# Causal mask moved from TensorE matmuls into VectorE's extreme pass, and the last group's product moved one step, in a fused attention and expert block

## The reference

```python
x = L0_attn_x                                  # [8, 1024, 256] f32
xn = _layernorm(x, axis=-1)
x = x + _L0_attn_ref(xn, w_qkv, w_out) + _L0_ffn_ref(xn, wg, w1, b1, w2, b2)

# attention: 16 heads of 64, 8 batches of 1024 tokens
logits = einsum('bqhd,bkhd->bhqk', q, k) / sqrt(64)
logits = where(tril, logits, -0.7 * finfo(float32).max)
probs = softmax(logits, axis=-1)
out = einsum('bhqk,bkhd->bqhd', probs, v)      # then einsum('bshd,hde->bse', out, w_out)
# _L0_ffn_ref: a top-2 mixture of 8 experts with capacity 2048, hidden size 1024
```

## Time and profile before

| | |
|---|---|
| median of three runs | 3558.74 us |
| profiled execution | 3556.85 us |
| its span | 3555.0 us |
| mean granted TensorE clock over the span | 0.982 |
| attention stage, from and to | about 935 to 3555 us |
| one unit | 40.2 us |
| busy in the span: PE, PEld, DVE, ACT, POOL | 95%, 78%, 62%, 59%, 40% |

### The profile page before, as it was taken

One profiled execution on the slowest core, in us unless ns is written; L12 is line 12 of the kernel. 1 busy time (PEld: TensorE's weight loads), 2 busy tenths in 40 slices (PEclk: granted clock), 3 DMA queues, 4 the chain that ended last, 5 costly groups with the idle time before them and its releaser, 6 DMA issues.

```text
span 3555.0 us, 67268 instructions
## 1 busy us (share of the span) xinstructions
PE 3390.4 (95%) x24085; PEld 2763.0 (78%) x24085; DVE 2219.5 (62%) x4719; ACT 2104.2 (59%) x4500; POOL 1436.5 (40%) x2025
## 2 busy tenths in 40 slices
PE   5599999999799999999999999999999999999998
PEld 3489998999677777777777777777777777777776
DVE  5844444443367666666666666667666666666666
ACT  2345444444366666666666666666666666666664
POOL 2122221220133345554454444554445444455445
PEclk8799999999899999999999999999999999999999
DMA  5122222221311112221222112211122111221111
GB/s 189 43 67 72 72 71 68 72 72 37 91 49 39 40 47 59 53 53 48 57 56 53 53 49 60 54 49 53 49 62 56 50 51 49 62 51 45 43 39 54
DMA packets 177498, 207.72 MB, mean 58 GB/s; under 512 B 50144, under 2 KB 150560, under 8 KB 177184
## 3 DMA queue, kind: packets, MB, share of 16 engines
q1 hardware_dynamic: 164896, 169.96, 17.2%
q0 software_dynamic: 12288, 33.57, 3.5%
HBM read 102.80 MB, written 33.55 MB: 38 GB/s over the span
## 4 chain that ended last, share of the span: by engine, by line
PE 46%; DVE 11%; POOL 7%; ACT 6%; issue 3%; ACTq 0%; POOLq 0%
PE S L1164 13%; PE T L1178 12%; PE O L1196 9%; DVE ql L1316 4%; DVE kk L1319 4%; PE S L1084 4%; PE W L1099 3%; PE W L1117 3%; ACT qh L1256 2%; POOL pr L1425 2%; POOL wl L1379 2%; ACT kk L1256 2%; POOL yg L1398 2%; DVE negm L1348 2%; ACT pr L1238 1%
## 5 line engine op out<-in xcount | busy, mean ns | idle before, releaser
L1425 POOL TENSOR_SCALAR pr<-pr,rinv 128x128 f32<-128x128 f32 (+7 forms) x1024 | 763.6, 747 | 1250.2 <-DVE rinv L1288 1247.3
L1238 ACT ACTIVATE pr<-S,negm 128x128 f32<-128x128 f32 (+7 forms) x1024 | 758.2, 740 | 555.5 <-DVE negm L1348 544.7
L1348 DVE TENSOR_REDUCE negm<-S 128x1 f32<-128x128 f32 (+7 forms) x1024 | 770.0, 753 | 228.1 <-PE S L1167 211.2
L1178 PE MATMUL T<-ident,pr 128*128 128x128 f32 x4608 | 697.7, 276 | 16.6 <-POOL pr L1425 11.2
L1196 PE MATMUL O<-pT,vv 128*64 128x256 f32 (+1 forms) x5120 | 584.2, 366 | 29.7 <-issue 29.5
L1164 PE MATMUL S<-kk,qh 128*128 128x256 f32 (+2 forms) x1536 | 590.1, 384 | 5.6 <-ACT pr L1238 5.6
L1226 ACT ACTIVATE pT<-T 128x512 f32<-128x512 f32 (+3 forms) x768 | 416.1, 542 | 263.8 <-PE T L1178 251.5
L1178 PEld LDWEIGHTS T<-ident,pr 128*128 128x128 f32 x4608 | 497.1, 141 | 41.2 <-POOL pr L1425 24.2
L1196 PEld LDWEIGHTS O<-pT,vv 128*64 128x64 f32 x5120 | 347.2, 137 | 219.3 <-issue 84.3
L1164 PE MATMUL S<-kk,ql 128*128 128x256 f32 (+2 forms) x1536 | 514.4, 342 | 0.0
L763 ACT ACTIVATE h<-pH,b1c 128x512 f32<-128x512 f32 x256 | 175.8, 687 | 364.6 <-PE pH L693 349.4
(11 more groups left out here) (189 smaller groups left out, 6491.0 us busy)
## 6 DMA issues: line engine op xcount, KB each, us to landing
qh<-qh SPq DMA_DIRECT2D x128, 256.0 KB
ql<-ql SPq DMA_DIRECT2D x128, 256.0 KB
y<-yb SPq DMA_DIRECT2D x128, 128.0 KB, 1.7
wr<-in_L_attn_w_qkv SPq DMA_DIRECT2D x128, 128.0 KB, 2.3
x<-in_L_attn_x SPq DMA_DIRECT2D x16, 512.0 KB, 5.4
xn<-xn SPq DMA_DIRECT2D x16, 512.0 KB, 5.4
w1r<-in_L_ffn_w SPq DMA_DIRECT2D x8, 1024.0 KB
w2r<-in_L_ffn_w SPq DMA_DIRECT2D x8, 1024.0 KB
```

Source lines behind the costliest of these rows:

```text
L1178: ins = e.transpose(T[ch % 2][:, b * P:(b + 1) * P], pr[s % RING][:, kt * P:(kt + 1) * P], k["ident"][:])
L1238: e.activation(pr[i][:, 0:w], S[s % 2][:, off:off + w], ACT.Exp, bias=negm[:, i:i + 1], accum_out=rsum[:, i:i + 1]).then_inc(expd.sem, 1)
L1348: e.tensor_reduce(negm[:, i:i + 1], S[s % 2][:, off:off + w], AX.X, ALU.max, negate=True).then_inc(negmax.sem, 1)
L1425: e.tensor_scalar(pr[i][:, 0:width(s)], pr[i][:, 0:width(s)], rinv[:, i:i + 1], 1.0, ALU.mult, ALU.mult).then_inc(scaled.sem, 1)
```

## The change

The scores are computed negated: q is scaled by -1/8 instead of 1/8. The mask matmul is gone. VectorE's pass over `S` adds a tile `late` (zeros, and +2.37e38 above the diagonal in its last 128 columns), writes the sum back into `S`, and takes its minimum, which is the `negm` that ScalarE needs; ScalarE's exponential has scale -1. `late` is filled once, by GpSimd, at the start of the attention stage; two constants of the first stage go. Group 3's product starts at step 4 instead of 3, and o3 moves from step 6 to step 7.

```diff
-    for name, dt in (("ident", F32), ("identb", BF16), ("mask", BF16), ("below", BF16), ("ones", BF16)):
+    for name, dt in (("ident", F32), ("below", BF16), ("ones", BF16)):
...
-            g.memset(t["identb"][:], 0.0)
-            g.memset(t["mask"][:], 0.0)
...
-            for name in ("ident", "identb"):
-                g.affine_select(t[name][:], t[name][:], [[-1, P]], ALU.not_equal, 1.0, base=0, channel_multiplier=1)
-
-            g.affine_select(t["mask"][:], t["mask"][:], [[-1, P]], ALU.is_ge, MASKED, base=0, channel_multiplier=1)
+            g.affine_select(t["ident"][:], t["ident"][:], [[-1, P]], ALU.not_equal, 1.0, base=0, channel_multiplier=1)
...
-    STEP_OF = {"q0": 0, "q1": 1, "k0": 1, "k1": 2, "o2": 2, "xn": 4, "v0": 5, "o3": 6, "v1": 7, "o0": 9, "o1": 13}
+    STEP_OF = {"q0": 0, "q1": 1, "k0": 1, "k1": 2, "o2": 2, "xn": 4, "v0": 5, "v1": 7, "o3": 7, "o0": 9, "o1": 13}
...
+        late = sb("late", [P, SEQ])
...
+                e.memset(late[:], 0.0).then_inc(s_late, 1)
+                e.wait_ge(s_late, 1)
+                e.affine_select(late[:, SEQ - P:], late[:, SEQ - P:], [[-1, P]], ALU.is_ge, -MASKED, base=0,
+                                channel_multiplier=1).then_inc(s_late, 1)
+                e.wait_ge(s_late, 2)
...
+        AFTER = [4 * g + 3 + LAG + 1 + (g == GROUPS - 1) for g in range(GROUPS)]
...
-                    part = s + d * STEPS - (4 * g + 3 + LAG + 1)
+                    part = s + d * STEPS - AFTER[g]
...
-        END = [(UNITS, s) for s in range(LAG + GROUPS)]
+        END = [(UNITS, s) for s in range(LAG + GROUPS + 1)]
...
-                    diag = off + i * P
-                    here = a <= diag < b
                     for t in (qh, ql):
                         ins = e.matmul(S[s % 2][:, a:b], t[q][h][:, i * P:(i + 1) * P], kk[q][h][:, a - off:b - off],
-                                       start=(t is qh), stop=(t is ql and not here))
-                    if here:
-                        ins = e.matmul(S[s % 2][:, diag:diag + P], k["identb"][:], k["mask"][:], start=False, stop=True)
+                                       start=(t is qh), stop=(t is ql))
...
-                e.activation(pr[i][:, 0:w], S[s % 2][:, off:off + w], ACT.Exp, bias=negm[:, i:i + 1],
+                e.activation(pr[i][:, 0:w], S[s % 2][:, off:off + w], ACT.Exp, bias=negm[:, i:i + 1], scale=-1.0,
...
-                    dst, scale = (qh, QSCALE) if name[0] == "q" else (kk, 1.0)
+                    dst, scale = (qh, -QSCALE) if name[0] == "q" else (kk, 1.0)
...
-                            ins = e.scalar_tensor_tensor(ql[to][h][hs, cols], W[hs, :], QSCALE,
+                            ins = e.scalar_tensor_tensor(ql[to][h][hs, cols], W[hs, :], -QSCALE,
...
-                    e.tensor_reduce(negm[:, i:i + 1], S[s % 2][:, off:off + w], AX.X, ALU.max,
-                                    negate=True).then_inc(negmax.sem, 1)
+                    masked = S[s % 2][:, off:off + w]
+                    e.tensor_tensor_reduce(masked, masked, late[:, SEQ - w:], 1.0, -MASKED, ALU.add, ALU.min,
+                                           negm[:, i:i + 1]).then_inc(negmax.sem, 1)
```

More of the change, by code:

```diff
@@ L917, in attention_and_sum @@
             s_xn = [psem(f"s_xn{i}") for i in loads]
-            s_tr, s_hi, s_lo = (psem(n) for n in ("s_ptr", "s_phi", "s_plo"))
+            s_tr, s_hi, s_lo, s_late = (psem(n) for n in ("s_ptr", "s_phi", "s_plo", "s_late"))
             wo_raw = res[:, QT:2 * QT, :]
```

## The result

The changed kernel takes 3605.39 us (median of 4 runs, 3601.74 to 3608.85) against 3557.92 us (3552.89 to 3559.75) for the kernel before: a ratio of 1.0136, interval 1.0118 to 1.0153. It is 47.5 us slower; the forecast was 3613, 54 us more than the 3558.74 of before. The profiled execution is the one of 3601.74 us, 44.9 us above that of before.

A forecast was written before the change was run, and what follows sets the result against it. TensorE bounds the unit, with the serial ScalarE/VectorE chain to exp(3) 0.5 us behind. +0.50 + 5 x per unit, +0.9 us at x = 0.08, times 63 is +57; less 1 for one-time effects: 3613 us, range 3552 to 3700.

The forecast's parts named there:

- The masks: TensorE loses 16 mask matmuls per unit, 0.07 to 0.08 us each, 1.1 us of its work per unit.
- The pass: VectorE's pass gains an SBUF input, a PSUM write and a minimum accumulator, each pass costing more than a `tensor_reduce`.
- x: Extra cost of one VectorE pass over a `tensor_reduce` of the same width: 0.005 to 0.2 us, taken as 0.08.
- rival D: VectorE's accumulating pass runs at half rate: some 5 us more per unit, about 3900 us; chance 0.04.
- Group 3: Its second part, 1.66 us, moves behind scores(5); TensorE idles 2 us and more before scores(4) and scores(5).
- The sum: Unit after: 13.15 + 3 x + 27.39 + 0.2 + 2 x = 40.74 + 5 x, against 40.24 us.
- The further 0.1 us of every other unit: At x = 0.2, ScalarE's late copy of v0 may cost every other unit 0.1 us more: 3655 us.
- The lower bound: With x = 0.005 and masks at 0.08 us, +0.35 us per unit, 3578 us in all.
- A, TensorE stays the bound: The chain gives way and all savings come off: 1.9 us per unit, 120 us, 3437 us; chance 0.13.
- B, no change: Time within 0.2%; needs x near -0.1 or twice the saving per mask; chance 0.05.
- C, the clock: New gaps lower TensorE's clock: 2 us more per unit, about 3740 us, less if only some units; chance 0.14.

The follow-up runs named there:

- the fastest version: Against the changed kernel: group 3's product and o3 at their old steps, GpSimd's weight split one step later, `xn` and `o2` at step 3; 3489.59 us.
- the two kernels with the later split: GpSimd's weight split at step 4 instead of 3, against the masks' move alone (3495.22 us) and against the kernel before (3536.54 us).
- the delay on the chain and off it: Changed kernel plus 256-column VectorE memsets ahead of the pass, at steps 1 to 3 (on, 3660.91 us) or 5 to 7 (off, 3611.69 us).

## Why the prediction was right

**The masks.** 0.07 to 0.08 us each, 1.1 us a unit. As TensorE's work that is nearly borne out: 39.68 us busy in a unit before, 38.70 in the fastest version's. As time of the unit it is less: the two kernels with the later split differ in the masks alone, and their units in 0.73 us (39.95 and 39.22). Of the rest, 0.16 is a longer wait in front of group 3's product (PE O on issue, 36.8 us in 58 times against 27.1 in 57, from 1100 to 3400 us), and from T(4) to scores(12), where the forecast had said that the masks bring nothing, four of them brought 0.07.

**The pass.** x was bounded by 0.005 and 0.2 and taken at 0.08; it is 0.065. The groups by form of the changed kernel (DVE, 965 to 3555 and 1000 to 3500 us):

```profile
L1351 DVE CUSTOM_DVE_ANT_0 S<-S,late 128x512 f32<-128x512 f32 x127 | 87.6, 690 | 2.5 <-PE S L1168 2.5
```
```profile
L1351 DVE DVE_READ_ACCUMULATOR2_ANT negm<- 128x1 f32 x976 | 137.9, 141 | 0.0
...
L1351 DVE CUSTOM_DVE_ANT_0 S<-S,late 128x1024 f32<-128x1024 f32 x122 | 150.4, 1233 | 14.5 <-PE S L1168 14.5
```

The pass at 512 columns takes 690 ns against the reduction's 686: the lower bound was the price of the main instruction. The rest is the second instruction, the accumulator's read. It is recorded with 141 ns and starts 0.08 us before the pass ends (2571.32, with the pass from 2570.98 for 0.42), so it adds 0.06. The Trainium skill, "VectorE: DVE Perf Modes", section "Two Vector instructions with no wait between them", has the two instructions; the trace agrees, with one read for each of the 1024 passes. The nearest row, ScalarE's read of 195 ns that shows 0.1, was a good guide. That VectorE has 8.9 us to spare in a unit was misread: 8.9 is what the 31.30 of PEld leaves in the earlier trace rows; VectorE's own 27.68 leave 12.6. Nothing in the sum hangs on it; in rival D it does, since D's 9.6 us would have fitted into VectorE's idle time.

**Group 3.** Both idle pieces were forecast in place and size: 0.7 and 1.5 us, measured 0.67 and 1.47. "O on issue" is gone and T(4) doesn't wait, as forecast, if for another reason than I gave: it was to come at about the same time as before, and it comes 0.4 us later (19.6 us after the first exponential, against 19.20), when GpSimd is done. The wait that went was worth a little more than 0.24: 0.29 in the kernel before, by the later split. This term carries the result, and the delay on the chain and off it bears it out.

**The sum.** Forecast 40.74 + 5 x a unit, 41.1 at x = 0.08; measured 40.97. Of the 0.17 us between 0.90 and 0.73, 0.08 is x. Nearly all the rest lies behind scores(5): from there to the next unit's first exponential it is 26.46 us against 25.47 before, +0.99, where the steps gave 0.97 + 2 x = 1.10. The kernel with the product's move alone has 27.02 there. So that move gave +1.55, where the forecast added 1.85 and took off 0.24, and the masks' gave -0.56, where it had -0.84 + 0.2 + 2 x = -0.51: half of the 0.11 each.

In the whole: the 63 units took 46.3 us longer (63 x 0.73 = 46.0), the stage began 2.0 us earlier, and the end took 0.5 longer: 44.9, against the forecast's 56. The units were not quite the same 63 times, as the forecast took them: the seven full ones without a gather were 39.95 before and grew by 1.02, and the first got 0.75 shorter, which about makes up for it. The further 0.1 us of every other unit didn't come: ScalarE does wait for v0 (42.7 us, 29 times, in the waits above), and all units but the first, the last and three of 41.2 are 40.97 long within 0.06. The lower bound was off by a little: by its own terms x = 0.005 and masks at 0.08 make 0.50 + 0.03 - 0.12 = +0.41 a unit and not +0.35, 3 us of 3578.

**The rivals.** A, TensorE stays the bound: fell, scores(5) wait in every unit. It needed the chain to have 0.5 us more room; the version with the product in its old place and the split later has TensorE as the bound nearly throughout, and there the gain exists. Its mechanism was right and its place in this kernel wrong. B, no change: fell. C, the clock: fell for this kernel; gaps of 0.67 and 1.47 us, 2.8 us apart, left it at 1.00 from 1300 to 3475 us. How close it was, the kernel with the delay on the chain shows: gaps of 1.17 and 1.94 us, and around and behind the second a granted clock of 0.81 and 0.85 in windows of 5 us, and the same in three more of its units. So the forecast's ground against C, that its gaps lie under the bound for idle gaps, doesn't hold as it stands: gaps under 2 us were enough there. D, half rate: fell, 1233 ns at 1024 columns and not over 2 us.

What I had not seen is how the two halves stand to each other: I summed them and did not say that the masks' move is a gain and the product's the loss, nor that the gain, alone, is held up at GpSimd's queue.

## What to carry to other kernels

When an engine is busy 98%, look at what it covers: the slack between its work and the serial chain behind its next wait (0.5 us here) is the most that may be taken or moved away from in front of that wait. Of a piece that is moved, follow its instructions on every engine, in the order of each queue: one that waits for another engine delays all behind it, and a wait that the profile shows with 0.6 us may give back 0.8.

## What the runs showed of the hardware that I had not expected

Writing the masked scores back to PSUM cost next to nothing: 690 ns at 512 columns with a second input from SBUF and the write, 686 ns for the reduction that only reads. The accumulator's read has a duration of 141 ns in the records and adds less than half of it. A `memset` of 256 columns on VectorE took 272 ns and cost the chain 0.26 us each, nearly all of it. In the kernel with the delay on the chain, two idle pieces of under 2 us, some 3 us apart, were followed by a lower granted clock in four units, and not in others with the same pieces.
